# The state's share of y in the first mixer, made over channels in y's own banks

## The reference

```
proj = layernorm(x) @ in_proj_w.T
gate, hBC, dt = split(proj, [1024, 1024 + 1152])
h, B, C = split(silu(conv4(hBC)))          # 1024, 64 and 64 channels
dt = softplus(dt + dt_bias);  a = -exp(A_log) * dt
# in chunks of time, A_cs = running sum of a within the chunk, per head
Y_diag = ((C B^T) * exp(A_cs[l] - A_cs[s]) for s <= l) @ (h * dt)
Y_off  = exp(A_cs[l]) * (C[l] @ state)     # what the state before the chunk gives
state  = exp(A_cs[last]) * state + B^T @ (exp(A_cs[last] - A_cs) * h * dt)
y = Y_diag + Y_off + D * h
out = rms_norm(y * silu(gate)) * norm_w @ out_proj_w.T
```

## Time and profile before

| | |
|---|---|
| median of three runs | 2891.32 us (2890.04 to 2891.45) |
| profiled execution | 2891.2 us, its span 2889.5 us |
| TensorE busy | 2754.8 us, 95% |
| VectorE busy | 1996.4 us, 69% |
| ScalarE busy | 1537.2 us, 53% |
| GpSimd busy | 927.3 us, 32% |
| mean granted clock of TensorE | 0.979 |

### The profile page before, as it was taken

The page is one execution under the profiler, slowest core; times in us unless marked ns, Lnnn a source line. Parts: engine busy times, 40 slices in busy tenths (PEclk is TensorE's granted clock), DMA queues, the critical chain, the costliest instruction groups (busy, mean ns, idle before and its releaser), DMA issues. The chain is left out here.

```text
span 2889.5 us, 49994 instructions
## 1 busy us (share of the span) xinstructions
PE 2754.8 (95%) x17464; PEld 1847.8 (64%) x17464; DVE 1996.4 (69%) x3695; ACT 1537.2 (53%) x2418; POOL 927.3 (32%) x614
## 2 busy tenths in 40 slices
PE   7999999999999999996999999999999999997996
PEld 6777776676766665455666666666666666664454
DVE  5666666666656664377787778888888877885267
ACT  3444444444445542342567666766667776664242
POOL 2222223322222331232333444333433334332134
PEclk9999999999999999998999999999999999998998
DMA  4000000000000034145000000000000000022333
GB/s 124 23 22 22 22 22 22 22 29 29 22 22 22 15 118 153 44 146 202 12 23 22 22 22 18 18 22 22 15 16 20 22 22 22 15 94 84 116 117 131
DMA packets 79935, 139.59 MB, mean 48 GB/s; under 512 B 17896, under 2 KB 17896, under 8 KB 78832
## 3 DMA queue, kind: packets, MB, share of 16 engines
q1 hardware_dynamic: 70752, 125.92, 12.7%
q10 hardware_dynamic: 9104, 12.63, 1.4%
HBM read 104.98 MB, written 33.55 MB: 48 GB/s over the span
## 5 line engine op out<-in xcount | busy, mean ns | idle before, releaser
L653 PE MATMUL work<-b_xnT,shared_w 128*128 128x256 f32 x2304 | 545.3, 388 | 2.3 <-DVE b_state L1234 1.4
L653 PE MATMUL work<-a_xnT,shared_w 128*128 128x256 f32 x2176 | 507.9, 391 | 1.3
L653 PEld LDWEIGHTS work<-b_xnT,shared_w 128*128 128x128 f32 x2304 | 426.1, 191 | 90.2 <-issue 30.3
L653 PEld LDWEIGHTS work<-a_xnT,shared_w 128*128 128x128 f32 x2176 | 417.6, 195 | 73.6 <-issue 12.3
L1219 DVE TENSOR_TENSOR b_decay<-b_decay,b_gt 128x1024 f32<-128x1024 f32 x256 | 350.3, 1390 | 119.2 <-ACT b_decay L932 115.7
L925 ACT ACTIVATE b_decay<-seg 128x1024 f32<-128x1024 f32 x256 | 248.5, 1029 | 113.2 <-PE seg L772 113.0
L932 ACT ACTIVATE b_decay<-b_decay 128x1024 f32<-128x1024 f32 x256 | 266.2, 1073 | 0.0
L1393 POOL TENSOR_TENSOR b_rhs<-b_l_side,of_head 128x1024 fp32r<-128x1024 f32 x32 | 82.0, 2562 | 550.4 <-DVE b_l_side L1188 550.4
L1428 POOL TENSOR_TENSOR a_y<-a_y,a_skip 128x1024 f32<-128x1024 f32 x32 | 91.0, 2843 | 495.2 <-DVE a_y L1208 495.2
L1098 DVE SCALAR_TENSOR_TENSOR shared_cv<-shared_pre,b_conv_w,shared_cv 128x256 f32<-128x256 f32 x480 | 230.9, 515 | 14.2 <-ACT shared_cv L869 6.3
L1098 DVE SCALAR_TENSOR_TENSOR shared_cv<-shared_pre,a_conv_w,shared_cv 128x256 f32<-128x256 f32 x432 | 189.7, 482 | 72.5 <-ACT shared_cv L869 66.8
(11 more groups left out here) (314 smaller groups left out, 4620.1 us busy)
## 6 DMA issues: line engine op xcount, KB each, us to landing
shared_x<-in_L_attn_a_x SPq DMA_DIRECT2D x16, 512.0 KB, 3.5
a_x_res<-in_L_attn_a_x SPq DMA_DIRECT2D x32, 256.0 KB, 2.6
x_mid<-a_x_res SPq DMA_DIRECT2D x32, 256.0 KB, 2.1
shared_w<-in_L_ffn_d_w SPq DMA_DIRECT2D x2, 4096.0 KB, 13.7
f_d_w<-in_L_ffn_d_w SPq DMA_DIRECT2D x2, 4096.0 KB, 15.0
f_x_res<-x_mid SPq DMA_DIRECT2D x8, 1024.0 KB, 5.6
f_bc_w<-x_mid SPq DMA_DIRECT2D x8, 1024.0 KB, 5.6
shared_x<-x_mid SPq DMA_DIRECT2D x16, 512.0 KB, 3.6
```

The source lines that it names most:

```text
L653: mm = nc.tensor.matmul(dst, w_in[:, k, col:col + m], xnT[:, k, :], start=(k == 0), stop=(k == KD - 1))
```

## The change

All of it holds for mixer A alone (`FOLD`).

- `yoff` gets no work bank any more. `csum` (`row_sums`) makes the running sums of all heads over the state's 128 rows in `seg`'s first pair of banks, `row_decay` takes their exponent into `cdec`, `decay_c` multiplies that by C (`cc`, C on both halves of the partitions), and `yoff` (`from_state_channels`) multiplies the state by it, with channels as rows, straight into y's banks: 16 matmuls of 64 by 64 by 128 per tile, which open the sum there. `ident` and `y1` are gone.
- D times h is made by GpSimd over channels (`xd`), and the gate becomes an addition of `xd` and a multiplication by silu(gate), four instructions in place of two per tile.
- The order changes: in the head `prs` stands in front of `zzb`, `seg0.0` and `yoff0` stand behind `xnT1`; in tile 1 `csum1`, `rt0`, `out0` come first and `seg1.0`, `yoff1` after them. `blk0` stands in front of `dt`. ScalarE and VectorE follow that order: `slot_mult` stands behind `out_add` in both tiles. `small_sums` and `next_decays` stay behind `slot_mult`.
- New waits: `seg` waits for `row_decay`, `yoff` for `decay_c` and for y's banks (`y_taken`), the state's decay on GpSimd for `yoff`, `xd` for `y_taken`, the gate for `xd`.

```diff
 blocks = [f"blk{b}" for b in range(NB)]
-fill0, fill1 = spread(["dt"] + blocks, NS), spread(["z1", "z2"], NS)
+fill0 = spread((blocks[:1] + ["dt"] + blocks[1:]) if FOLD else (["dt"] + blocks), NS)
+fill1 = spread(["z1", "z2"], NS)
 if NP > 2:
...
 def head(prev, nxt):
+    if FOLD:
+        return (["zza", "xT0", "xT1", "xT2", "xT3"] + b_and_g + ["csum0"] + (["prs"] if prev else []) + ["zzb"]
+                + (["prt"] if prev else []) + (["xnT0"] if nxt else []) + (["pout"] if prev else [])
+                + (["xnT1"] if nxt else []) + ["seg0.0", "yoff0", "small1"])
     return (["zza", "xT0", "xT1", "xT2", "xT3"] + b_and_g + ["zzb"]
...
 steps += ["z0a", "z0b"] if nxt else []
-steps += ["rs0", "yoff1a", "yoff1b", "seg1.0", "rt0", "out0"]
+steps += ["rs0", "csum1", "rt0", "out0", "seg1.0", "yoff1"] if FOLD else \
+    ["rs0", "yoff1a", "yoff1b", "seg1.0", "rt0", "out0"]
 for p in range(NP):
...
     steps += (["small0"] if nxt else []) + state_steps(1)
-if p == 0:
+if p == 0 and not FOLD:
     steps += ["ident1"]
...
     pe.wait_ge(state_ready, FREE + 2 * (2 * i + j))
-    if FOLD:
-        c_half = bcs[N:P, 0, j * P:(j + 1) * P] if q else bcs[0:N, 1, j * P:(j + 1) * P]
-        mm = nc.tensor.matmul(bank[:, :], c_half, state[q * N:(q + 1) * N, :], start=True, stop=True)
-    else:
-        mm = nc.tensor.matmul(bank[:, :], bcs[0:N, 1, j * P:(j + 1) * P],
-                              state[0:N, q * 512:(q + 1) * 512], start=True, stop=True)
+    mm = nc.tensor.matmul(bank[:, :], bcs[0:N, 1, j * P:(j + 1) * P],
+                          state[0:N, q * 512:(q + 1) * 512], start=True, stop=True)
 elif name[:5] == "state":
...
 pe.wait_ge(seg_taken, FREE + tile * NS + 2 * p)
+if FOLD:
+    pe.wait_ge(cs_exp_done, tile + 1)
 for k in range(4):
...
+def row_sums(tile):
+    pe.wait_ge(rhs_ready[0], tile + 1)
+    pe.wait_ge(seg_taken, FREE + tile * NS)
+    for half in range(2):
+        rows = slice(half * 64, half * 64 + 64)
+        mm = nc.tensor.matmul(seg[0][:, half * 512:(half + 1) * 512], l_ones[rows, :],
+                              rhs[0][rows, 4 * half:4 * half + 4, :].rearrange("p h l -> p (h l)"),
+                              start=True, stop=True)
+    mm.then_inc(cs_full, 1)
+def from_state_channels(tile):
+    pe.wait_ge(setup_v, 1)
+    pe.wait_ge(cdec_ready, FREE + tile + 1)
+    pe.wait_ge(state_ready, FREE + 2 * tile)
+    pe.wait_ge(y_taken, FREE + 2 * tile)
+    for b in range(4):
+        for s in range(2):
+            for q in range(2):
+                mm = nc.tensor.matmul(ybank[64 * q:64 * q + 64, (4 * s + b) * P:(4 * s + b + 1) * P],
+                                      state[s * N:(s + 1) * N, (2 * b + q) * HP:(2 * b + q + 1) * HP],
+                                      cdec[s * N:(s + 1) * N, 4 * q + b, :],
+                                      start=(b == 0), stop=False, skip_group_check=True)
+    mm.then_inc(yoff_done, 1)
...
 act.wait_ge(xt_ready, FREE + 4 * n)
+if FOLD:
+    act.wait_ge(skip_done, FREE + 2 * n)
 nc.scalar.activation(xs[:], cv[:, 0:KE, :], ACT.Silu).then_inc(silu_done, 1)
-act.wait_ge(y1_ready, FREE + 4 * n)
+if FOLD:
+    act.wait_ge(cdec_ready, FREE + 2 * n)
+    for q in range(2):
+        nc.scalar.activation(cc[q * N:(q + 1) * N, :], cv[N:P, KE, :], ACT.Silu)
+else:
+    act.wait_ge(y1_ready, FREE + 4 * n)
 if FOLD:
...
 gate_silu(i)
+if FOLD:
+    row_decay(2 * i)
+    if prev:
+        out_rsqrt(2 * i - 1)
+    if nxt:
+        xnT_copy(sec, 0)
+        xnT_copy(sec, 1)
 slot_bound(sec, 0, 0)
...
 slot_exp(sec, 0, 0)
-if prev:
+if prev and not FOLD:
     out_rsqrt(2 * i - 1)
-if nxt:
+if nxt and not FOLD:
     xnT_copy(sec, 0)
 slot_exp(sec, 0, 1)
-if nxt:
+if nxt and not FOLD:
     xnT_copy(sec, 1)
...
     z_copy(sec, "z0b")
+if FOLD:
+    row_decay(2 * i + 1)
+    out_rsqrt(2 * i)
 slot_bound(sec, 1, 0)
...
 slot_exp(sec, 1, 1)
-out_rsqrt(2 * i)
+if not FOLD:
+    out_rsqrt(2 * i)
 for p in range(NP):
...
+def decay_c(sec, j):
+    tile = 2 * sec.i + j
+    dve.wait_ge(cs_exp_done, tile + 1)
+    c8 = cc[:, j * P:(j + 1) * P].unsqueeze(1).to_broadcast([P, 8, P])
+    if j == 0:
+        dve.wait_ge(kcol_ready, sec.i + 1)
+        nc.vector.scalar_tensor_tensor(out=cdec[:], in0=cdec[:], scalar=kcol[:], in1=c8, op0=ALU.mult,
+                                       op1=ALU.mult).then_inc(cdec_ready, 1)
+    else:
+        nc.vector.tensor_tensor(cdec[:], cdec[:], c8, ALU.mult).then_inc(cdec_ready, 1)
...
 dve.wait_ge(sq_done, FREE + 2 * tile)
+if FOLD:
+    dve.wait_ge(skip_done, FREE + tile + 1)
+    for half in range(2):
+        dve.wait_ge(ydiag_done, FREE + 2 + tile * NS + (half + 1) * (NS // 2))
+        cols = slice(half * 4, half * 4 + 4)
+        nc.vector.tensor_tensor(
+            yz[:, cols, :], ybank[:, half * 512:(half + 1) * 512].rearrange("p (b t) -> p b t", b=4),
+            xd[:, cols, :], ALU.add).then_inc(y_taken, 1)
+    for half in range(2):
+        dve.wait_ge(y_taken, FREE + 2 * tile + half + 1)
+        cols = slice(half * 4, half * 4 + 4)
+        nc.vector.tensor_tensor(yz[:, cols, :], yz[:, cols, :], zs[:, cols, j * P:(j + 1) * P], ALU.mult
+                                ).then_inc(yz_done, 1)
+    return
 for half in range(2):
...
     square_sums(sec, "prs")
-from_state(sec, 0)
+if not FOLD:
+    from_state(sec, 0)
 if prev:
...
 make_xdt(sec, 1)
+if FOLD:
+    if prev:
+        out_scale(2 * i - 1)
+    decay_c(sec, 0)
+    if prev:
+        out_add(sec, "pout", i - 1, 1)
 slot_mult(sec, 0, 0)
-if prev:
+if prev and not FOLD:
     out_scale(2 * i - 1)
 slot_mult(sec, 0, 1)
-if prev:
+if prev and not FOLD:
     out_add(sec, "pout", i - 1, 1)
...
 square_sums(sec, "rs0")
-from_state(sec, 1)
-rms_var(sec, "rt0")
+if FOLD:
+    rms_var(sec, "rt0")
+    out_scale(2 * i)
+    decay_c(sec, 1)
+    out_add(sec, "out0", i, 0)
+else:
+    from_state(sec, 1)
+    rms_var(sec, "rt0")
 slot_mult(sec, 1, 0)
 slot_mult(sec, 1, 1)
-out_scale(2 * i)
-out_add(sec, "out0", i, 0)
+if not FOLD:
+    out_scale(2 * i)
+    out_add(sec, "out0", i, 0)
 if nxt:
...
 dve.wait_ge(small_loaded, 16 * 5)
+if FOLD:
+    for r in range(0, P, 32):
+        own, other = (slice(0, N), slice(N, P)) if r % 64 == 0 else (slice(N, P), slice(0, N))
+        nc.vector.tensor_scalar(l_ones[r:r + 32, own], ones[r:r + 32, own], c["l_row"][r:r + 32], None,
+                                ALU.mult)
+        nc.vector.tensor_scalar(l_ones[r:r + 32, other], ones[r:r + 32, other], 0.0, None, ALU.mult)
+    for q in range(2):
+        nc.vector.tensor_copy(d_chan[q * N:(q + 1) * N, :], d_skip[q * N:(q + 1) * N, :].rearrange(
+            "p (b q) -> p b q", q=2)[:, :, q])
 link(nc.vector.tensor_scalar(a_low[:], a_log[:], 44.0, None, ALU.min))
...
         pool.wait_ge(folded, FREE + i + 1)
-pool.wait_ge(xt_ready, FREE + 4 * i + 2 * j + 2)
-nc.gpsimd.tensor_tensor(skip[:].rearrange("p (h q) -> p h q", h=H),
-                        xt[:, j, :].rearrange("p (h q) -> p h q", h=H),
-                        d_skip[:].unsqueeze(2).to_broadcast([P, H, HP]), ALU.mult
-                        ).then_inc(skip_done, 1)
-pool.wait_ge(y1_ready, FREE + 2 * tile + 2)
-pool.wait_ge(skip_done, FREE + tile + 1)
-nc.gpsimd.tensor_tensor(y1[:], y1[:], skip[:], ALU.add).then_inc(y1x_ready, 1)
+if FOLD:
+    pool.wait_ge(silu_done, FREE + 2 * i + 1)
+    pool.wait_ge(y_taken, FREE + 2 * tile)
+    nc.gpsimd.tensor_tensor(xd[:], xs[:, :, j * P:(j + 1) * P],
+                            d_chan[:].unsqueeze(2).to_broadcast([P, KE, P]), ALU.mult
+                            ).then_inc(skip_done, 1)
+else:
+    pool.wait_ge(xt_ready, FREE + 4 * i + 2 * j + 2)
+    nc.gpsimd.tensor_tensor(skip[:].rearrange("p (h q) -> p h q", h=H),
+                            xt[:, j, :].rearrange("p (h q) -> p h q", h=H),
+                            d_skip[:].unsqueeze(2).to_broadcast([P, H, HP]), ALU.mult
+                            ).then_inc(skip_done, 1)
+    pool.wait_ge(y1_ready, FREE + 2 * tile + 2)
+    pool.wait_ge(skip_done, FREE + tile + 1)
+    nc.gpsimd.tensor_tensor(y1[:], y1[:], skip[:], ALU.add).then_inc(y1x_ready, 1)
 pool.wait_ge(xdt_done, FREE + tile + 1)
...
 pool.wait_ge(xw_ready, FREE + tile + 1)
+if FOLD:
+    pool.wait_ge(yoff_done, FREE + tile + 1)
 by_head = state[:].rearrange("p (h q) -> p h q", q=HP)
...
 pool.wait_ge(small_loaded, 16 * 5)
+pool.wait_ge(setup_v, 1)
 tile_steps(0, 0)
```

More of the change, by code:

```diff
@@ L359, in mixer_phase @@
         decay = sb("decay", [P, DECAYS, 8, P])
-        y1 = sb("y1", [P, E])
-        skip = sb("skip", [P, E])
+        if FOLD:
+            cc, cdec, xd = sb("cc", [P, SUP]), sb("cdec", [P, 8, P]), sb("xd", [P, KE, P])
+            l_ones, d_chan = sb("l_ones", [P, P], F32R), sb("d_chan", [P, KE])
+        else:
+            y1 = sb("y1", [P, E])
+            skip = sb("skip", [P, E])
         xw = sb("xw", [P, E])
@@ L411, in mixer_phase @@
         folded = sig("folded")
+        cs_full, cs_exp_done, cdec_ready = sig("cs_full"), sig("cs_exp_done"), sig("cdec_ready")
```

(21 more changed lines are left out.)

## The result

The changed kernel takes 3065.26 us (median of four runs, 3064.14 to 3070.17) against 2890.70 for the kernel before. The ratio is 1.0601, with a 95% interval of 1.0588 to 1.0614: 6.0% slower. The profiled execution has a span of 3063.2 us, 173.7 more than before. All of it arises in mixer A: from its first steady supertile on (125.42 there, 121.57 before) to its last one (1226.82 there, 1066.09 before) it is 156.8 us, ahead of that 3.9, behind it 13.0. Mixer B takes as long as before: its first and last `b_lhs` (an operand of its `seg`) are made at 1556.0 and 2785.9 here, at 1383.2 and 2614.3 before.

A forecast was written before the change was run, and what follows sets the result against it. TensorE, busy 95% of the span, was taken to bound the kernel. 14 steady supertiles at +7.7 us make 108, with the ends 122, with clock 136: 2891 + 136 = 3027 us, range 2958 to 3075.

The forecast's parts named there:

- `BG` to `dt`: Head and tile 0 on TensorE: `dt` waits for the bank that `small_sums` frees; +3.4 us for the same work.
- gate of tile 0, `z0a` to `rs0`: Gate of tile 0: two additions now come first on VectorE, so `rs0` starts later; +1.1 us.
- the lock: VectorE's second gate multiplication waits out GpSimd's `xd`, and the state's decay reaches into `slot_mult`: together +2.3 us, 0 to 2.9.
- `rs0` to `sums`: Tile 1: `sums` waits for VectorE's `next_decays`; 15.35 us from `rs0` against 13.5 before, +1.9.
- behind `sums`: Tile 1, after `sums`: `ident1` is gone, -1.0 us per supertile.
- clock: TensorE, wait before thin `dt`: one short fall per supertile, 1.7 us less 0.7 for existing falls; +1.0, between 0 and 4.2.
- The chain behind `seg`: Bounds, exponents and multiplications after `seg` come into the open: waits of 2.9 us before `dt`, 1.5 before `sums`.
- its small part: Each tile: the state's decay on GpSimd, now behind `yoff`, reaches into the first `slot_mult`; 0.2 us each, 0 to 0.5.
- `yoff`: TensorE, each tile: the new `yoff`, 32 instructions of 128 columns and 64 outputs, takes 1.5 us, ends 1.15 and 1.9.
- The long-clock rival: Every supertile loses 4.2 us to the clock, as the first did before the change: 3072 us, chance 0.15.
- Ends: First and last supertile of mixer A: about +6 us and about +8 us, together +14.
- the rival *faster: TensorE keeps its cover and only work counts: 20 us saved, 29 if `yoff` takes 1.15; 2866 us, chance 0.05.

The follow-up runs named there:

- xd_late: Changed kernel with GpSimd's `xd` waiting for the gate's end (`yz_done`) instead of the end of its additions (`y_taken`): 2989.10 us.
- the best kernel: Changed kernel, `csum` in y's banks, `xd` at gate's end, `z0a` copied before squares, `out_add` between tile 0's `slot_mult`s, `seg1.0` between `rs0` and `rt0`: 2852.05 us.

## Why the prediction was right, and which term was off

The direction, the mechanism and the place and releaser of all four waits were as forecast; 3027 was said and 3065 measured, inside the range of 2958 to 3075 but near its upper end. The steps, laid at full clock beside what the profile after shows (the slow stretches taken off by their rows: 1.69 of `zzb`, and 1.69 of the eight blocks, 15.75 against 14.06 in the run with the waits filled):

| step | forecast | measured |
|---|---|---|
| `BG` to `dt` (measured from `zza`) | +3.4, with the lock +3.6 | +3.1 |
| gate of tile 0, `z0a` to `rs0` | +1.1, with the lock +3.0 | +2.75 |
| `rs0` to `sums` | +1.9, with the lock +2.1 | +1.3 |
| behind `sums` | -1.0 | -1.3 |
| sum | +7.7 | +5.9 |
| clock | +1.0 | +5.3 |
| supertile | +8.7 | +11.2 |

From `zza` to `dt` it is 385.06 - 358.36 - 1.69 = 25.01, for 477.29 - 455.36 = 21.93 before. From `z0a` to `rs0` it is 411.70 - 405.30 = 6.40, for 499.47 - 495.82 = 3.65 before; from `rs0` to `sums` it is 426.53 - 411.70 = 14.83, for 13.5. `z0a` before:

```profile
495.82 3.72 PE L653 MATMUL work<-a_xnT,shared_w 128*128 128x256 f32 x16
```

The supertile is (1226.82 - 125.42) / 14 = 78.67 against (1066.09 - 121.57) / 14 = 67.47. The clock's part is the difference, and the filled waits measured it independently: 74 us, 4.9 per supertile. Per supertile the waits were forecast 1.8 too long and the clock 4.3 too small; over 14 supertiles that is 25 us one way and 60 the other, so the 3027 would have been 3002 with the waits as they were. That it missed by no more than 38 is in part luck.

- **The chain behind `seg`.** Right: `dt` waited 2.74 (forecast 2.9), released by `small_sums`; `sums` waited 1.24 (1.5) for `next_decays`. Moving either reader removed its wait, and moving `seg` in the old kernel made both (2.9 and 2.3).
- **`prs` before `zzb`.** Right: 1.46 for 1.26.
- **GpSimd's lock in the gate.** Right, shown by the run xd_late: 2.98 against 1.28 for the two multiplications. The second alone took 2.29 (2.98 less the 0.69 of the first), 2.5 was forecast. But its small part, the state's decay reaching into `slot_mult`, did not happen. It took 1.04 alone and was over at 381.25, before `slot_mult` began at 382.00, so the +0.4 for that wasn't there. In the kernel before, beside VectorE, it had taken 1.91:

```profile
471.47 1.91 POOL L1445 TENSOR_TENSOR a_state<-a_state,a_e_fold 128x512 f32<-128x512 f32 x1
```

- **`yoff`.** 1.10 busy, below my low end of 1.15; I had taken 1.5. That is 34 ns per instruction on 64 rows and 64 columns of the array, where `ydiag`, on 128 rows and 64 columns, has 60. In tile 0 it didn't matter, the wait took it up, as said.
- **The clock.** This is the term that was mis-sized: +1.0, bounds 0 and 4.2, measured 5.3 by difference and 4.9 by filling, above its upper bound. The step reads "I take one short fall per supertile" at the one wait before `dt`. No row of the prediction shows its 1.7 for a short fall, but the trace of the kernel before does: nine blocks that take 15.79 took 17.47 in another supertile.

```profile
677.68 17.47 PE L653 MATMUL work<-a_xnT,shared_w 128*128 128x256 f32 x72
```

So the size of one fall was right, and their number was not. The runs show that closing any of the four waits gave clock back, and that filling the one before `rs0` gave more than filling that before `dt`. Even `zzb`, behind the wait of 1.46, took 3.68 for 1.99 in the supertile shown. The long-clock rival, at 4.2 and 3072 us, was nearer to what happened than the forecast; the loss had another shape, though, several falls of which the shown supertile has two of 1.69. The supertile of 78.67 lies outside the 74 to 76 that the prediction names as a sign.
- **Ends.** +17 for +14.
- **A slip.** In the rival *faster*, a `yoff` of 1.15 saves 5.12 - 0.88 - 2.3 = 1.94 per supertile and not 1.8, or 31 us in place of 29. It changes no chance.

## What to carry to other kernels

Where TensorE's own order bounds a kernel as here, a chain through the other engines is free only while a long stretch of matmuls runs beside it; before a step is moved, look at which long matmul covers the chain that starts with it, and where each reader's place in its queue is. Price a new wait of TensorE at more than its length, since it can take the clock with it. Closed alone, these waits gave 1.9 to 3.0 times their length; all four together, 8.11 us of waits, cost 5.3 more in clock, 1.65 times. Filling a wait with matmuls that nobody reads tells what its clock costs. A buffer that forces an order is worth a search for another bank, but look at the order first. Here four changes of order turned +6.0% into -0.8% with the running sums where they were; moving them to other banks, with the readers back in their old order, made it -1.0%, and two more changes of order -1.4%.

## What the hardware showed that I had not expected

- Waits of TensorE of 1.2 to 2.7 us, four in 78 us with dense work between, held its mean clock at 0.92; filled with matmuls whose results nobody reads, the same order ran at 0.99 and 74 us faster.
- VectorE's wait for GpSimd isn't kept to operations with two tensors from SBUF. In the best kernel a tensor-by-column operation of 128 columns took 1.92 where it takes 0.34, beside GpSimd's `xd`. It does so once in every steady supertile; the one of the other tile, with no `xd` beside it, takes 0.34.

```profile
504.16 1.92 DVE L1252 TENSOR_SCALAR a_lhs<-a_parts,s_row,l_row 128x128 fp32r<-128x128 f32 x1
```

```profile
504.06 1.93 POOL L1532 TENSOR_TENSOR a_xd<-a_xs,a_d_chan 128x1024 f32<-128x1024 f32 x1 [3.65 <-DVE a_yz L1326]
```

- A row of GpSimd's taken while VectorE was busy can hold a wait: the state's decay took 1.91 in the kernel before and 1.04 when nothing ran beside it. VectorE's multiplication of 469.76 ended there at 472.48, and 1.04 from that is 473.52, near the decay's end at 473.38. That the difference is a wait is an estimate from these numbers.
